# One element of the batch passes the local attention alone: a two-layer fp32 model on one core, with its order of work redrawn

## The reference

```python
xn = layernorm(x)                        # "layer 0"
x  = x + gla(xn) + local_transformer(xn)
xn = layernorm(x)                        # "layer 1"
x  = x + delta(xn) + switchhead(xn)
```

## Time and profile before

| what | value |
|---|---|
| median of 3 runs | 1239.53 us (1236.46 to 1243.86) |
| the profiled execution, its own time | 1239.64 us |
| its span in the profile | 1238.2 us |
| busy share: TensorE matmuls, TensorE weight loads | 94%, 75% |
| busy share: VectorE, ScalarE, GpSimdE | 74%, 57%, 68% |
| read from HBM | 225.71 MB, 185 GB/s over the span |

### The profile page before, as it was taken

One profiled execution on the slowest core, in us unless ns is written; L12 is line 12 of the kernel. 1 busy time (PEld: TensorE's weight loads), 2 busy tenths in 40 slices (PEclk: granted clock), 3 DMA queues, 4 the chain that ended last, 5 costly groups with the idle time before them and its releaser, 6 DMA issues.

```text
span 1238.2 us, 31062 instructions
## 1 busy us (share of the span) xinstructions
PE 1161.1 (94%) x11890; PEld 922.5 (75%) x11890; DVE 913.7 (74%) x1902; ACT 707.2 (57%) x2020; POOL 840.4 (68%) x1156
## 2 busy tenths in 40 slices
PE   5887789999999999999999999999999999899998
PEld 3454458877778788787887877987788877788786
DVE  4958786986888978885687787986677766784534
ACT  5787877656756564467645665457775533332322
POOL 3745467687688845799488726798669736873871
PEclk9889989999999999999999999999999999999999
DMA  7101165654366665773477556685257666777763
GB/s 267 35 23 52 33 225 183 211 193 157 117 192 206 208 198 172 250 253 115 168 234 242 180 165 197 230 280 165 94 161 228 227 205 242 237 249 250 262 225 125
DMA packets 91186, 230.87 MB, mean 186 GB/s; under 512 B 9888, under 2 KB 16160, under 8 KB 90912
## 3 DMA queue, kind: packets, MB, share of 16 engines
q1 hardware_dynamic: 90896, 228.30, 56.3%
q10 hardware_dynamic: 144, 0.59, 0.1%
HBM read 225.71 MB, written 3.15 MB: 185 GB/s over the span
## 4 chain that ended last, share of the span: by engine, by line
PE 57%; DVE 22%; ACT 10%; issue 4%; DMA 3%; POOL 2%; DVEq 0%; SPq 0%; ACTq 0%; POOLq 0%
PE bank L948 13%; PE bank L901 12%; PE bank L612 5%; PE bank L829 4%; DVE ogate L1358 4%; PE bank L938 3%; PE bank L919 3%; DVE dy L1211 2%; PE bank L647 2%; PE bank L929 2%; DMA kv<-values 2%; DVE kv L1125 2%; PE bank L671 2%; ACT prob L1469 2%; PE bank L657 1%
## 5 line engine op out<-in xcount | busy, mean ns | idle before, releaser
L1744 POOL TENSOR_TENSOR vgate<-vgate,xT 128x512 f32<-128x512 f32 x256 | 325.7, 1298 | 72.0 <-DMA vgate<-gates 67.3
L901 PE MATMUL bank<-wv,vgate 128*128 128x128 f32 x2048 | 252.6, 277 | 1.6 <-POOL vgate L1744 1.0
L901 PEld LDWEIGHTS bank<-wv,vgate 128*128 128x128 f32 x2048 | 242.4, 192 | 13.4 <-issue 7.8
L948 PE MATMUL bank<-ogate,wo 128*128 128x256 f32 x1024 | 242.7, 383 | 2.1 <-DVE ogate L1358 1.7
L948 PEld LDWEIGHTS bank<-ogate,wo 128*128 128x128 f32 x1024 | 188.5, 190 | 33.0 <-issue 8.9
L1358 DVE TENSOR_TENSOR ogate<-ogate,bank 128x1024 f32<-128x1024 f32 x128 | 153.4, 1212 | 34.6 <-PE bank L938 28.3
L1469 ACT ACTIVATE prob<-prob,mx 128x128 f32<-128x128 f32 (+1 forms) x256 | 96.0, 377 | 47.6 <-DVE mx L1061 47.2
L1628 ACT ACTIVATE mprob<-bank,mmin 128x256 f32<-128x256 f32 x128 | 59.4, 469 | 107.5 <-DVE mmin L1347 106.9
L1676 POOL TENSOR_TENSOR rot<-rot 128x512 f32<-128x512 f32 x64 | 82.0, 1281 | 55.2 <-DVE rot L1037 54.9
L612 PE MATMUL bank<-wqkv,hT 128*128 128x512 f32 x192 | 107.0, 661 | 2.9 <-ACT hT L1405 1.9
L1721 POOL TENSOR_TENSOR dlt<-dlt,step 128x126 f32<-128x126 f32 (+22 forms) x248 | 93.3, 376 | 19.4
(11 more groups left out here) (224 smaller groups left out, 2385.5 us busy)
## 6 DMA issues: line engine op xcount, KB each, us to landing
ogate<-gates SPq DMA_DIRECT2D x128, 512.0 KB, 4.2
vgate<-gates SPq DMA_DIRECT2D x128, 512.0 KB, 4.0
wo<-in_wo_moe SPq DMA_DIRECT2D x128, 256.0 KB, 4.6
wv<-in_wv_moe SPq DMA_DIRECT2D x128, 256.0 KB, 4.5
kv<-values SPq DMA_DIRECT2D x64, 256.0 KB, 4.7
local<-in_local SPq DMA_DIRECT2D x1, 1715.0 KB, 9.4
wqkv<-in_wqkv SPq DMA_DIRECT2D x2, 768.0 KB, 6.4
x<-in_x SPq DMA_DIRECT2D x8, 128.0 KB, 5.3
```

The source lines that it names most:

```text
L901: i = nc.tensor.matmul(out[:, n * D:(n + 1) * D], xg[:, e, n * P:(n + 1) * P], m.wv[slot][:, e, :], start=(q, n, e) == (0, 0, 0), stop=(q, ...
L948: i = nc.tensor.matmul(out[:, 0:T], m.wo[slot][:, e, :], cg[:, e, :], start=(h, q, e) == (0, 0, 0), stop=(h, q, e) == (MH - 1, 1, EQ - 1))
L1744: i = tt(gate[:, e:e + half, :], gate[:, e:e + half, :], spread(m.xT[b % 2][:, :], 1, half), ALU.mult)
```

## The change

`layers_in_turn()` before: blocks go in pairs of elements, (0,0), (1,0), (0,1), (1,1), then the same for elements 2 and 3, 4 and 5, 6 and 7. After: element 0's two blocks come first, by themselves; then elements 1 and 2 as a pair, 3 and 4, 5 and 6; element 7's two blocks are last. All five strings of turns and the string of banks are new. No stage and no instruction is added or removed, and each stream has as many letters as before.

```diff
 def layers_in_turn():
 
-    return [(b + i, l) for b in range(0, NB, 2) for l in range(DEPTH) for i in range(2)]
+    alone, pairs = [(0,)], [(b, b + 1) for b in range(1, NB - 1, 2)] + [(NB - 1,)]
+    return [(b, l) for group in alone + pairs for l in range(DEPTH) for b in group]
```

The beginning of TensorE's string (two of twelve lines; the rest, and the other strings, differ in the same way):

```diff
 TENSOR_TURNS = (
-    "GaaaaGGGaaaaaXabbabbaGbbbaababGbbabacaaacbGbGGaccabGcbbaaabbGbGbGaabGbaaabbbcabacbbbcbcbbGcbbaGbacacGaaaacacbG"
-    "GbacbzabaGaCaACaAbGFGbGaaGAaCababbabbabbbcVaFVaVAAaAcabVPcAFVcAAcAPzbbVbaPaACabaPbbCGGVbbFbbVAAbcAabaPcaVbbVbA"
+    "GaaaaGGGaaaaaXabbabbaGbbbbGbbbGbcGGcGccGcaaaaaaaabbababbbabaaaGGGbbaabbbcaacabbaGccabGcbbbbGzabababbabGGcaaGcCa"
+    "aaccbabACGcGGbaAGFbbbaaaCAbbbaabbaaabbVcabVacVAAbFAPcFcAPcVaaaAAbPAbaPaaAaabVGGVbFbbAAbbAbacbaPcbPbGaVcAVbbDbV"
```

And of SyncE's, whose first `C` is the write of element 0's gates and is not followed by the same loads (`o` for output gates, `v` for value gates):

```diff
 SYNC_TURNS = (
-    "xxxGGGGGGGGGGGGGGGGGGGGGGGCooovvvvvvvovovooGGGGvvovvovvCoovvoovvoooooGGGGGvvvGGvvGGvvvoExooovvvoovvoovooCGvvGG"
+    "xxxGGGGGGGGGGGGGGGGGGGGGGGCvvvooovvvoovoovGGGGvoovvvvoovvooCvvoovvoooGGGGGvvvGGvvGGvvvvoEoxoovvovvooovCvoGvGG"
```

More of the change, by code:

```diff
@@ new lines @@
+    "DVDDbDGVDDbAcAVcAGDVcVcADDPcEGGPPGzPAAVACVaFaaaCPPPAAaaAVaaaAVaPbPbaaabbabACAbbbPbAVFVFbAaaaaaAPAAaGAGVbDaFAGD"
+    "VGbPcDADAcDDbPDbcADDPcbDPcADDbAADbbDDPADbbbDDVDVbbADDbDAcVDDcADVcAcGGVVDDAcPzPEPAAVCACFPVPaaAAAPCAaVVPAaAAaVPA"
+    "aFFFPaAaAAVAaVDPabPbDVaDGaaaAbDGAAbAPaaaaabbbPVaAbDVabDDGDDbbDAbDbcAbDAcDbDDVcDGADDVcDPcDDbDAADDbbbDGAGGGbbVPV"
+    "AbbDDbPcAAPAVEcPPcAVcAGAVAPaGcaaaAVAAGPaaAVaPVAaAAaAPGGPVGAPAAbbAaPGazDbaaaVbbDPaabaaaVCAVaAADFaACbDbPbGDVAbbA"
+    "ADbDPcADDGcDVDDCDPAcDDPcADbcDbFDDPDDbDADFAFDDVVAGbADAPbbEAbDPbbAVVPAAbbAbPcAVcVPcAcAVcAPVAzGPACAGCFPAVVaPCaaVV"
@@ L122 @@
[L122 to L128 removed]
+    "VaaaaaGaaaaaaGbGGGbbGGbbGGbbGGbGGGGGGccGcGcccGcaaaaaabaaabbbabbbaabGaaGGGaacGGcabacGbbGGbGGcccGaGbcaGGbbGGbzCa"
@@ new lines @@
+    "aCaaGcccaaGabcccaGbbcCCCbACCCCbACGFbFaabGaabGGGaaGGaabGcGFbbcVVFbOOAcFAFccccVVaaOOaaAbAbaabaabaVVGGOGOAGAcbGGb"
+    "cabcGGbFFbDDVbVbFObVVODAcccAczCCOOcCCCCCCCCVVAcaAcaFFaaOOVVGAFAFcccDGcaOOAVVaAOOAFFAaaGDDDbGFDFbbGDGDbbVDVGGDb"
+    "GDODbDODAbGAGDGDFDVDVGDGGGDGGcGGcVVADcDADVVcccDDcEDOGzCGOaCaOOAVVFaaACCCaaCCOaaOCaaAVVCbACbbFabbaFbObOFbaaVVFF"
+    "DAAaaaaOOAGADFFDDVVFGGGDcGDODcbcDObbDAGbGGAGDcccGcDbODODbADbADbDVVDDOOcDcDcDVDAVAcccGVVGDDGcGDzCEOCOAGCCCCCCCA"
+    "aCVaOVOaaGAGGAFVVFFOOFaaAFFAFFaaaDOODAVVFbaDDAbbDVVbaaDOaaOAbaaAbbaabDVVDDGDODbOcbbADcDbcADDGVVccDccDbDODODbbD"
@@ new lines @@
+    "AGbAGGDVVGGDDGGGDcOOAEcAGcGVVcccOaOaAGGAGGcaaGGaaOVVOGGAaAaVVaOOAaAGGObODbbGADzCbaaCaaDDbAVaabVaaVVODOFADbCCAC"
+    "DbCCCCOODCFcDAFDcAVDVDFcDcccODbDcObDbFDDbDFAFDAFDVVFDbGOObGEAbDDAGDbGGVVGGGGOAOAcccVVOOccccAAVVzCCOOCCCCCCCCaa"
+    "VVGGAGGAGaGaVGVGODOaaAFAFFaaVVaObOAbFADbabDDFODOADbAVDVbDbDbDGDaDacDacDacGDcDccDOODcDaaAFDbDAGVbbDVabaDDFFFObD"
+    "bbVVOEbGAGGAGGGGGGcOzcAcOACVVCccccOOaaAaaAVVaaDaabAOObbAFbFFCVVCbACAVVbbOCCDbCODDACCDAVVODOFcGGGGcDOcODADFADVV"
+    "FGGDGcDGccDcODOAFFVDVAFDDODVDOVDGDDAGVVADDDGEzCCOOVAVACCCCOOCAVVCACCOOAFAFFDOODDDFVVAAFDFFFDOODVVFVDVADADDDDOD"
@@ new lines @@
+    "OVDVADADDDDDODOADDAVVDEOOVVAAOOAAVVOOAAVVOOAADOODDDADADVDVDDODOVDVADADDDDODOVDADADDDOOE")
+SCALAR_TURNS = (
+    "GaaaGaGGaGaaaaaaaXaabaabbbbbbbbbbbcGcGGccaaaaaaaaaaabaaabbaaabbbabaGGGbbaGbbabaaaacaacbacabacbaabbbabbbaCbbaba"
+    "GGacaacaGcaCaacbaACbbaGaaGAaGbbAbaCAGaabbbaaaabbaaabaabcaFbFaAcbFAcAFcAaaaaAaAaAabbAabaaababbaAbbbaAAcbaacabbc"
+    "AFbbbbAcbbAbAAbCbCCcAaCAcAacAaAGGaaAFAcFAGaaAAAAFAaAaAFaAGaGaaGbGaFbbbbbAbbbAAbAbbcAcADAcDcAEGGGCAaCaAaCaaAAaa"
+    "aaAaaaaaaAbaaAabbAbbbFbbFaaFbAaabFCaAaAaAaaAaaGaAbAaAGFGbGcAcbcbAcbAAabbbAAbbbAbbAbcAcDDcAcAAECACCAaAAaAaCaaAA"
+    "AaFAaFaFAaFAaAAFaaaAaabaAbaAbaaAaaaaaAbaaAbbbaaabAabGbbGbbAcbcAbAcGAcbbbADGbGAbbGAGDAbbbAcEAcAcAcAaAaAaAaaAaaa"
+    "aAaAaAaAAGGAaaGAAbaaabaCbAaaaaaabaaAabbACaaAaaCAbAbbGAbbAbcAGFcAFCAccbaFbbAFADAFDAGbAEbGbAbAbbAAbbbAAcAcccAAAA"
+    "CCACaCaaAAAaaaAaAAaaAaFaAaabAaFAabFAAbAbbbAabAbbGGbbabaaccGacaacaAaaAFDbADabbAaGaGaFabbbEbbAGbGAbAbbAcAcAcACcA"
+    "aACaaaAaaAaaAaaaAaabAabAaACbFAbAbbAbAbbAbAbAbAFcCccAFAAFcAAAFAAGGADDGAAEACACAACAAAAAACAAAFAFAAFAFFAAAAAAAADADA"
+    "AEAAAAAAAAAAAAAAAAAAAAAAAAAAAADDAE")
@@ new lines @@
+GPSIMD_TURNS = (
+    "aaaaaaaaGbGbGGbGbGGGGaaaaaaababbabaaaGaGaabaGbGGGbGGbaaaaaGaababbaaabaWaaWaaWbGGbWWWGGaWaaabaaWbaaWGGbGGbWWbDW"
+    "WbDDDDWWDaDaaDWWaDGaWWaaaDbDDbGDWbDDDWDGbDDGDGDWDDGWGWDGGWWWDDDDDaDaaaWaaWaaDbWabWbDbaDaaWGaaaWaWWDDGDDbDbGGDG"
+    "DDbDDDbDWDDWDWWGDWWDDDDWWDaaaDaWDWaaDaWaWGWGbGDbWaaaDaabaabaDWDDWDDbDDbDDGWDWDDDbbWGDGWDDDGGWDWGaGaWaaWDaGaGDD"
+    "aaDGWbWWaabaaWaabaaWDDbDDDDDDDDDWbDWbDDDWWWbDGDbDWWDDWWGGWGDWDDWWGaaaGDWWaaGGaaWaWbbDWDDbDDWbDDaDaDaDGDaWDDDDa"
+    "abWbaaDDbbDDDWDDWWaDaaaDaWaaaGbGGWbGWWWbWWbWDDGGDDDWDWGDDGDWDDWDWDWDDWWGDWWDDDDDDDDWWWWWDWDWDDWDWDDDDDWDDWDDDW"
+    "DWDDWDDWDWDWDDWWWDDDDDWDWDDDDDDDDD")
@@ L145 @@
[L145 to L148, removed]
+    "76543210765204375642356073425603245603241560372415603724513762405137602541305415741630574301057641056710456741"
@@ new lines @@
+    "16723641237451374275124571234375146352751364521742417572417247417347167517465714651461575416745167542167541062"
+    "75104675106750146705146705461706174474171734137417016431437601437601460171604317403147731407310471031705714054"
+    "71507450715467103541605173457345732014573014530153015473015430713540731543150745107140573714703147104705407543"
+    "75413135345343547335364735673476536756473156704352670325107321563256130276513026305126057320657236275032675301"
+    "7635240736154706134506731457631547065175604157601470165")
```

58 lines of the change are left out of this document (16 added, 42 removed).

## The result

The changed kernel takes 1286.0 us (median of its undisturbed runs, 1280.79 to 1287.49) against 1239.19 us (1236.46 to 1243.86): a ratio of 1.0345, 95% interval 1.0305 to 1.0386, slower by 3.4%. The forecast was 1239, no change. One run of 2304.74 us was disturbed and is left out. The profiled execution took 1284.51 us with a span of 1283.2, 45 us more than the span before. From here on "opening" means the part up to the first value matmul of element 0 (L901, after the change L902, as every line behind 245 is one higher).

A forecast was written before the change was run, and what follows sets the result against it. TensorE, busy 94% of the span, was taken as the bound, the opening being held by chains of few layers in fixed-order engines. Opening 0 and dense part -1 on 1239.64 gave 1239 us, no change; 8 in 10 range 1226 to 1253.

The forecast's parts named there:

- x of element 0 at 119: Opening: element 0 alone ends its second layer at 119 us (114 to 125) against 132.7, ready 14 us earlier.
- The savings named for the lone first layer: Element 0's first back: gaps of 1.1 and 3.0 us and some 0.5 before the layernorm go; x at 64.5.
- TensorE's clock, at most 3 us: Opening: six projections of the lone second front at the low clock throughout add 3 us, within the bounds.
- The gates 38 us after x: Opening: ScalarE's remaining 33 us of work takes 38 us (33 to 41), so the gates are sent at 157.
- The loads, -4: SyncE's queue after the gates' write: value pairs issued first bring the first expert matmul 4 us sooner (0 to -6).
- Work ahead, +3.8: TensorE: 3.8 us of work no longer stands ahead of the first expert matmul and must come later.
- Opening 0 (-10 to +10): Up to the first expert matmul: gates at 157, that matmul at 171, -4 + 3.8 = 0.
- rival 2: Opening: the lone layer leaves an unfilled hole, expert matmuls start at 180, 1250 us in all; chance 0.21.
- Dense part -1 (-8 to +8): Behind the opening: up to 2 us gained from VectorE's lighter load, 1 us lost to tighter backs.
- the 8 named as the sign of being wrong: Behind the opening: TensorE's idle time changing by over 8 us would show the forecast wrong.
- Rival 3: Tight backs: opening even, hidden and down projection stall TensorE 0.5 us a back, +6 to +8, 1246 us; chance 0.06.
- Rival 4: Behind 177 us TensorE is not the bound; better mixing of chains could take 1%, 1228 us; chance 0.04.

The follow-up runs named there:

- fill_after: The changed kernel with 92 matmuls that nothing reads added on TensorE ahead of 46 waits: 16.5 us faster than the changed kernel (14.6 by the ratios).
- fill_again_new: The new pairing, its order improved by small moves, with 59 matmuls that nothing reads added: 8 us faster than without them (7 by the ratios).
- load_after: The changed kernel with only SyncE's string altered, three pairs of output gates and weights issued ahead of the three value pairs: 1287.64 us against 1286.0.
- fill_open_after: The changed kernel with only the 68 unread matmuls that stand in its first 195 us: 1281.53 us against 1286.0.
- the moved orders: Orders of both pairings, changed by small moves from each pairing's own order; new pairing 1245 to 1263 us, worst old one 1245.11.
- the two fresh draws: All six strings drawn anew by one list scheduler for each pairing: old pairing 1325.92 us against 1242.09 before; the new pairing's 26 us above the old one's.

## Why the prediction was wrong

*x of element 0 at 119 (the step that failed first).* Its bounds were 114 to 125; measured 131.9. The chain in its parts, in us, with fill_after for the same order at nearly the full clock:

| part of element 0's chain | forecast | after | fill_after |
|---|---|---|---|
| first output projection starts | 50.0 | 52.4 | 50.5 |
| to x of the first layer | 14.5 | 17.3 | 13.6 |
| to the second layer's first scores | 15.5 | 12.7 | 12.7 |
| to its output projection | 22 to 24 | 26.8 | 25.2 |
| to x of the second layer (the back) | 16 to 19 | 22.7 | 22.8 |
| x of element 0 ready | 119 | 131.9 | 124.7 |

Two prices were missing. The first is TensorE's own: 7.2 of the 13 us go when the clock is restored. The savings named for the lone first layer were there (ScalarE began the gelu's table load at 62.67, 2 us ahead of the earlier trace rows), but slow matmuls took them back, 1.8 us in the output projection and 1.8 in the hidden matmuls; with the clock restored the first layer's x comes at 64.0, where 64.5 was forecast. The second is VectorE's other work. The second back lasts as long at the full clock, so its slow hidden matmuls are not what made it long. VectorE has hardly a gap in it: before, after and fill_after, from the output projection to x:

```profile
113.56:132.70 19.14, 15.69 (x105) 9.02 (x103) 17.75 (x42) 15.29 (x40) 13.81 (x13) 1.00 0.10 27
```

```profile
109.20:131.90 22.70, 17.19 (x158) 11.42 (x158) 21.75 (x51) 16.73 (x47) 14.48 (x13) 0.92 0.22 60
```

```profile
101.89:124.66 22.77, 17.62 (x174) 12.55 (x174) 21.75 (x51) 16.80 (x47) 14.56 (x13) 1.00 0.22 57
```

The new order puts six pairs of the linear attention's scans (1.27 us a pair) on VectorE there, where before has three; VectorE is busy 4.0 us longer than before in the back, and the back is 3.6 us longer. Element 0 is not alone on that engine.

The holes of the lone chain show in the waits of TensorE for GpSimdE's rotary product (us in total, number, longest), before and then after:

```profile
PE bank L627 <- POOL rot L1683: 5.9, 7, 2.6
```

```profile
PE bank L628 <- POOL rot L1684: 15.8, 8, 4.1
```

*TensorE's clock, at most 3 us and "within the bounds" (the mis-sized term).* Both prices stood in the earlier trace rows; I applied them to six projections only, not to every matmul of a chain that can't run beside anything. fill_after puts the opening's part at 7 us, fill_again_new at 8.5. The Trainium skill's "TensorE: Matmul & The Clock Gate" has in its section HAM oscillation — how this bites in real kernels a kernel whose TensorE keeps falling back to half rate in its waits for DMA and pays for it in span. The trace agrees in kind, with waits for the other engines: the granted clock was 0.74 in 50 to 75 us, and restoring it won 7.2 us of opening.

*The gates 38 us after x (bounds 33 to 41).* Measured 131.9 to 171.29 = 39.4: right, and by the mechanism given. ScalarE's work up to the gates' matmul was 114.1 us (114 forecast), of which 35.9 were left at x (33 forecast), done at a rate of 0.91 (0.81 to 0.88 taken); the two small errors cancel. But the 81 us taken as done by 119 were not: 67.6 were. The late x sets the send at 171.3, behind the 166 that I gave as the bound.

*The loads, -4.* Right: load_after shows 4.2 at the first value matmul. From the gates' matmul to the first value matmul it took 15.0 us instead of 18.0; 14 was forecast.

*Work ahead, +3.8.* The count of records ahead of the first value matmul fell by 42, as forecast in kind. The clock hid it: TensorE was busy the same 131 us.

*Opening 0 (-10 to +10).* This sum counts the shift of the first value matmul and the work moved behind it. The shift was +11.5 (at most +6 was allowed), the work 3.8 (taken as forecast): +15, well outside. It is the mechanism of rival 2, a lone layer that leaves a hole, decided by a send later than 160. Its 1250 had +5 + 4 + 2; the shift was over twice its +5, and 7 us of it were the clock's, which it put at 2.

*Dense part -1 (-8 to +8): the larger failure, 30 us* (34 behind the first value matmul, less the 3.8 of work moved there). TensorE's idle time behind the opening rose by 13 us, over the 8 named as the sign of being wrong; most of the rest is busy time at a lower clock, and fill_open_after shows that lifting the clock alone did not win it back. I compared two orders by a few summed figures (VectorE's work in one window, gaps between parts of a back) and took what they did not show as equal. Rival 3 did not happen: TensorE's waits at the hidden matmuls were 3.6 us in all (four, 3.3 of them in the opening), and its listed waits name no down projection. VectorE in 372 to 434 went down to 53.2 us as forecast, and TensorE's idle time there went up, from 1.9 to 3.4:

```profile
372.00:434.00 62.00, 58.62 (x430) 46.49 (x429) 53.18 (x107) 35.13 (x98) 52.46 (x78) 0.98 0.62 209
```

That the order costs this much, and that the pairing need not, is what the moved orders show: behind the opening the new pairing loses 1 to 5 us. Which part of the order does it is open. Rival 4 (TensorE isn't the bound behind the opening) can't be told from these runs; TensorE's busy share there stayed at 95 to 98% in all kernels but the two fresh draws (92%).

## What to carry to other kernels

A change of grouping in a statically ordered program comes with a newly drawn order; price the two apart, by giving both groupings orders of the same quality, before the grouping is blamed or kept. Here the drawn order cost about 30 us and the grouping 12 to 17, most of it in the opening. A chain that runs alone must be priced with TensorE at 1.2 GHz at each of its steps, and with what the other engines' queues hold beside it. A few matmuls that nothing reads, placed in its waits, tell on the chip whether the clock or the waits cost: they gave back 7.2 and 8.5 us of opening with the lone layers, and 0.2 where two layers were in flight.
